# Batch-ahead routing and value sums collected by VectorE, in a recurrent block with attention and eight experts

## The chip, the cores and the metric

The kernel runs on one core of a Trainium2 chip. The metric is device time in microseconds. A core has TensorE (PE, with its weight loads shown as PEld), VectorE (DVE), ScalarE (ACT), GpSimd (POOL) and SyncE (SP), each with an instruction stream of its own; they meet at semaphores, and SyncE issues most of the transfers.

## The reference

Two layers on an input of 8 batches, 1024 positions and 256 features (8192 rows). Each layer is a sequence block times a gate, added to the input. The part that matters here is the gate of the second layer: attention with 16 heads of 8 dimensions within each batch, and a mixture of eight experts that routes each row to two of them.

```python
scores = jnp.einsum('bhsk,bhtk->bhst', Q[..., :KPH], K) / math.sqrt(KPH)
attn = jax.nn.softmax(scores, axis=-1)
ao = jnp.einsum('bhst,bhtv->bhsv', attn, V)
...
mla_out = ao @ o_w + o_b
probs = jax.nn.softmax(mla_out @ router_w + router_b, axis=-1)
topw, topi = jax.lax.top_k(probs, TOPK)          # TOPK = 2 of E = 8
topw = topw / (topw.sum(-1, keepdims=True) + 1e-08)
h1 = jnp.einsum('bsd,edf->ebsf', mla_out, w1) + b1[:, None, None, :]
h1 = jax.nn.gelu(h1, approximate=False)
h2 = jnp.einsum('ebsf,efd->ebsd', h1, w2) + b2[:, None, None, :]
moe_out = jnp.einsum('bse,ebsd->bsd', combine, h2)
```

The first layer's state-space scan and the second layer's delta rule are other stages of the same program; the change doesn't touch them.

## The kernel before

The program is a row of phases, each with a block of its own for every engine; one begins when the one before has ended. The phases in question are `attention` (from line 2008) and, within `experts`, `route` (from line 2356), followed by `compute` and `combine`.

**Attention** works in 32 units: a batch (8) times a group of four heads (4). Per unit PE makes twice the scores of four heads. First, the row maxima: 32 tiles of 128 queries by 1024 keys into the double-buffered `psM` (`maxima`, two matmuls of 512 columns each, L2172); VectorE reduces each to its maximum (`maximum`, L2321) and so frees the buffer. `minus_max` writes them as two parts, PE turns them (`turn`), ScalarE copies them (`turned`), SyncE puts them beside the queries, so that the second product is already reduced by the maximum. Then the scores themselves: 64 banks of 128 keys by 512 queries into three banks `psS` (`scores`, L2198); ScalarE exponentiates each into `probs` (`exponentials`, L2281) and so frees the bank. After each four banks PE adds `probs` times values into the one bank `psV` (`values`, L2211), in 16 groups of four, eight for each half of the queries. When a half is complete, `psV` is copied to `sums` (`collect`, L2286), and SyncE stores it (`store`). The next half's first `values` waits for `sums_ready`. The maxima run 8 tiles (`LEAD`) and one unit ahead of the scores. PE's order is fixed in `step`: for each s, maxima tile half 0, scores bank 2s, maxima half 1, scores bank 2s+1; after every second s the values of one group. ScalarE collects at position `MIDDLE` of a unit and at its end.

**Routing** takes 16 tiles of 512 rows, two to a batch. VectorE makes the inverse softmax sums (L2589), which go to memory and come back spread over the rows. Per tile SyncE fetches values and inverse sums (`values`, `inverses`, L2424, L2428), VectorE multiplies them (`tile`, L2602), PE turns the product and makes the logits (`tile`, L2548, L2550), ScalarE copies the turned rows (`tile`, L2500). Per batch: `choose` on VectorE (L2616 to L2635) makes the softmax, with the exponential by ScalarE (`exponential`, L2510), takes the two largest of eight and makes the mask; PE counts it (`ranks`, L2567, L2568); `spots` (L2641 to L2652) turns the counts into places `K.spot`; GpSimd scatters the rows there by 16 indirect transfers a batch (L2491). Beside it, one expert a batch, the weights are folded: SyncE fetches `raw1` and `raw2` (`weights_of`, 512 KB each, L2435, L2436), PE multiplies (`fold`: L2558 for the weights, 16 small products L2561 for the bias), ScalarE writes the heads (L2504, L2506) and VectorE the rests (L2606, L2608).

In each engine the order is written out. PE: two tiles, fold(b), ranks(b-1). ScalarE: two tiles, exponential(b-1), fold(b). VectorE: two tiles, fold(b-1), choose(b-1), spots(b-1). After the last batch VectorE makes the tables of expert tiles. SyncE has two raw buffers, so `weights_of(e)` from e = 2 waits for fold(e-2) of PE (`folded`) and VectorE (`rest2`).

## Time and profile before

| | us |
|---|---|
| median of 3 runs | 4166.02 |
| lowest, highest | 4165.89, 4167.23 |
| profiled execution, time | 4168.11 |
| profiled execution, span | 4166.5 |
| PE busy | 3502.2 (84%) |
| VectorE busy | 3253.8 (78%) |
| ScalarE busy | 2306.2 (55%) |
| GpSimd busy | 1369.6 (33%) |

The span is what the profile covers; the profiled execution's own time is 1.6 us above it. The busy time of an engine is the time in which it works on an instruction; the ends of matmuls are modelled, and matmuls of two kinds can overlap, so a busy PE is not a full PE. A timeline gives for each instruction, or a run of equal ones, the start, the time to the end of the run, and in brackets the idle time of the engine before it and what ended that. Such a releaser is inferred, and can be wrong where the named transfer had long landed.

### The profile page before, as it was taken

The page shows a single profiled execution, that of the slowest core. Times are in us where ns is not written, and L with a number is a line of the kernel's source. Part 1 is how long each engine was busy: PE and PEld are TensorE (multiplying, and loading weights), DVE is VectorE, ACT ScalarE, POOL GpSimd, SP SyncE. Part 2 cuts the span into 40 slices and gives each one's busy share as a digit, 9 for nine tenths or more (in the row PEclk, how much of TensorE's full clock was granted, in tenths as well). Part 3 has the DMA queues.
Part 4 walks back from the last instruction along what each step waited for, and adds up shares of the span by engine and source line. Part 5 has one row for each costly group of instructions (what it writes and reads, how often), then busy time and mean ns, then how long its engine had stood idle before and what let it go on. Part 6 is the DMA issues. An engine that isn't in the chain of part 4 may idle for free. (4 is left out here: it accounts for less than half of the span.)

```text
span 4166.5 us, 65564 instructions
## 1 busy us (share of the span) xinstructions
PE 3502.2 (84%) x20079; PEld 2104.2 (51%) x20080; DVE 3253.8 (78%) x4239; ACT 2306.2 (55%) x4128; POOL 1369.6 (33%) x905
## 2 busy tenths in 40 slices
PE   8969888888657979989799999999999965379950
PEld 3445555555346868878233333333333324279950
DVE  8959999999786645657889898989899823368868
ACT  6755555555594533311288888888888851033323
POOL 4448888889302445410000000000000004645530
PEclk9989999999888989999599999999999985589975
DMA  6665444454677943377123232322222114222348
GB/s 218 248 207 175 164 163 162 162 172 137 206 253 189 253 119 106 91 195 221 40 52 74 52 73 52 71 55 64 61 59 66 30 42 133 89 77 90 92 159 293
DMA packets 536067, 538.10 MB, mean 129 GB/s; under 512 B 85296, under 2 KB 441776, under 8 KB 535648
## 3 DMA queue, kind: packets, MB, share of 16 engines
q1 hardware_dynamic: 521856, 497.23, 40.8%
q0 software_dynamic: 13952, 37.74, 2.6%
q8 instruction: 123, 2.02, 0.2%
q14 instruction: 136, 1.11, 0.1%
HBM read 317.93 MB, written 215.71 MB: 128 GB/s over the span
## 5 line engine op out<-in xcount | busy, mean ns | idle before, releaser
L2321 DVE TENSOR_REDUCE at_top<-at_psM 128x1 f32<-128x1024 f32 x1024 | 1206.1, 1220 | 136.5 <-PE at_psM L2172 135.4
L2281 ACT ACTIVATE at_probs<-at_psS 128x512 f32<-128x512 f32 x2048 | 1060.9, 603 | 250.8 <-PE at_psS L2198 250.8
L2198 PE MATMUL at_psS<-at_q,at_k 64*128 64x512 f32 x2048 | 795.3, 468 | 8.3 <-ACT at_probs L2281 8.3
L575 POOL TENSOR_TENSOR sc_prod<-sc_state,sc_c_row 128x1024 f32<-128x1024 f32 x256 | 709.1, 2789 | 117.2 <-DVE sc_state L724 109.0
L2172 PE MATMUL at_psM<-at_k,at_q 62*128 62x512 f32 x2048 | 689.7, 451 | 36.5 <-DMA at_vraw<-scratch_vf 21.9
L724 DVE TENSOR_TENSOR_SCAN sc_state<-sc_dec,sc_psI 128x1024 f32<-128x1024 f32 x256 | 578.4, 2280 | 53.3 <-PE sc_psI L645 29.5
L2172 PEld LDWEIGHTS at_psM<-at_k,at_q 62*128 62x128 f32 x2048 | 313.1, 190 | 601.8 <-DVE at_top L2321 519.8
L2211 PE MATMUL at_psV<-at_probs,at_v 128*32 128x512 f32 x4096 | 546.3, 605 | 0.0
L656 PE MATMUL sc_psY<-sc_prod,sc_ident 128*128 128x512 f32 x1024 | 467.4, 597 | 3.5 <-DVE sc_y L710 2.2
L606 ACT ACTIVATE sc_dec<-sc_dt,sc_a_exp 128x1024 f32<-128x1024 f32 x256 | 293.6, 1148 | 311.1 <-DVE sc_state L724 308.3
L2198 PEld LDWEIGHTS at_psS<-at_q,at_k 64*128 64x128 f32 x2048 | 337.6, 184 | 195.5 <-ACT at_probs L2281 190.6
L2139 POOL COPY at_v<-at_vraw 128x256 f32<-128x256 f32 x32 | 12.9, 403 | 1253.1 <-DMA at_vraw<-scratch_vf 1169.4
L645 PE MATMUL sc_psI<-sc_diag,sc_uT 128*128 128x128 f32 x2048 | 266.9, 285 | 91.8 <-DVE sc_state L724 86.9
L645 PEld LDWEIGHTS sc_psI<-sc_diag,sc_uT 128*128 128x128 f32 x2048 | 245.6, 196 | 184.2 <-DVE sc_state L724 136.8
L656 PEld LDWEIGHTS sc_psY<-sc_prod,sc_ident 128*128 128x128 f32 x1024 | 185.6, 193 | 185.2 <-issue 173.1
L2765 POOL DMA_INDIRECT scratch_ys<-ex_y,ex_slot x156 | 172.0, 1103 | 185.1 <-DVE ex_y L2898 138.9
L2352 PEld LDWEIGHTS ex_psY<-ek_w,ex_hid 128*128 128x128 f32 x1872 | 223.8, 188 | 3.9 <-issue 1.0
L2352 PE MATMUL ex_psY<-ek_w,ex_hid 128*128 x1872 | 224.9, 279 | 0.6 <-DVE ex_hid L2891 0.6
L703 DVE TENSOR_TENSOR sc_psI<-sc_u,sc_b_row 128x1024 f32<-128x1024 f32 x128 | 171.1, 1337 | 8.7 <-ACT sc_uT L584 8.7
L2491 POOL DMA_INDIRECT scratch_xs<-er_rows,ek_spot x128 | 129.5, 1012 | 115.9 <-DVE ek_spot L2652 72.6
L592 ACT ACTIVATE sc_diag<-sc_ident,sc_b_col 128x128 f32<-128x128 f32 x512 | 161.7, 387 | 6.3 <-PE sc_psI L645 6.3
L2785 ACT ACTIVATE ex_xT<-ex_psT 128x512 fp32r<-128x512 f32 x39 | 23.4, 600 | 253.4 <-PE ex_psT L2815 253.4
(393 smaller groups left out, 4941.4 us busy)
## 6 DMA issues: line engine op xcount, KB each, us to landing
sc_c_row<-scratch_bc SPq DMA_DIRECT2D x128, 512.0 KB, 4.3
scratch_xs<-at_zeros SPq DMA_DIRECT2D x140, 264.0 KB, 4.7
sc_b_row<-scratch_bc SPq DMA_DIRECT2D x64, 512.0 KB, 5.1
ec_y<-scratch_ys SPq DMA_DIRECT2D x32, 512.0 KB, 6.4
ex_x<-scratch_xs SPq DMA_DIRECT2D x39, 264.0 KB, 3.1
si_x<-in_x SPq DMA_DIRECT2D x16, 512.0 KB, 4.4
scratch_xn<-si_xn SPq DMA_DIRECT2D x16, 512.0 KB, 5.1
scratch_x_t<-si_xT SPq DMA_DIRECT2D x16, 512.0 KB, 5.7
```

What stands on the lines that cost most here:

```text
L575: pool.tensor_tensor(prod[:, (n * H + h) % 8, :], state[slot][:], c_row[n % ROWS][:], ALU.mult).then_inc(prod_ready, 1)
L606: act.activation(dec[slot][:], dt[k][h][:], ACT.Exp, scale=a_exp[:, h, n:n + 1]).then_inc(dec_ready, 1)
L645: last = pe.matmul(psI[h][:, c, :], uT[k][h][:, c, :], diag[order % 2][:, c, :], start=True, stop=True)
L656: last = pe.matmul(psY[h][:, cols], ident[:], prod[:, own % 8, cols], start=(n == 0), stop=(n == S - 1))
L724: dve.tensor_tensor_scan(state[slot][:], dec[slot][:], psI[h][:].rearrange("p c t -> p (c t)"), 0.0, ALU.mult, ALU.add).then_inc(state_rea ...
L2172: ins = pe.matmul(psM[t % 2][:, half * TILE:(half + 1) * TILE], rows_of(q4[j], h, 0, MAXROW)[:, c * P:(c + 1) * P], rows_of(k4[j], h, 0, M ...
L2198: pe.matmul(psS[v % 3][:], rows_of(k4[j], h, 0, GROUP)[:, c * P:(c + 1) * P], rows_of(q4[j], h, 0, GROUP)[:, half * TILE:(half + 1) * TILE ...
L2211: last = pe.matmul(psV[32 * h:32 * h + 32, :], v4[j][:, c, h, :], probs[:, slot(j, at_slot[4 * g + n]), :], start=(c == 0), stop=(c == KC ...
L2281: act.activation(probs[:, slot(j, v), :], psS[v % 3][:], ACT.Exp).then_inc(act_done, 1)
L2321: dve.tensor_reduce(top[j % 2][:, h, c:c + 1], psM[t % 2][:], AX.X, ALU.max, negate=True).then_inc(maxed, 1)
L2352: last = pe.matmul(out, a, b, start=start and n == 0, stop=stop and n == len(parts) - 1)
L2765: pool.indirect_dma_start(out=A["ys"], out_offset=bass.IndirectOffsetOnAxis(ap=slot[par][:, s:s + 1], axis=0), in_=y[par][:, s, :], in_off ...
```

## The change

In attention, ScalarE's `collect` is taken out and given to VectorE, which does it ahead of maxima tile 26 (half 0, of the unit before) and tile 10 (half 1, of two units before), `COLLECTED`; the last three follow the loop. In routing, each engine turns the tiles of batch b+1 before batch b is chosen; PE's `fold` is split into the weights' product, ahead of ranks, and `fold_bias`, behind them; PE folds one batch later, ScalarE and VectorE two. There are three raw buffers instead of two. SyncE fetches the inverse sums of tiles 0 and 1 right after the first store of inverses, ahead of the first weights, and the later weights one tile later.

```diff
-    MIDDLE = at_slot[36]
+    COLLECTED = (18 + LEAD, FIRST + LEAD)
...
-                def collect(u, half):
-                    act.wait_ge(summed, u * GROUPS + (GROUPS + KC * (half + 1)))
-                    act.wait_ge(sums_st[half], u * QUAD * 16 + 16)
-                    act.activation(sums[half][:], psV[:], ACT.Copy).then_inc(sums_ready, 1)
...
-                            if e == MIDDLE:
-                                collect(u, 0)
...
-                        collect(u, 1)
...
+                def collect(u, half):
+                    dve.wait_ge(summed, u * GROUPS + (GROUPS + KC * (half + 1)))
+                    dve.wait_ge(sums_st[half], u * QUAD * 16 + 16)
+                    dve.tensor_copy(sums[half][:], psV[:]).then_inc(sums_ready, 1)
+
                 def unit(u, j):
                     for t in range(MT):
+                        for half in range(NHALF):
+                            back = half + 1
+                            if t == COLLECTED[half] and (not isinstance(u, int) or u >= back):
+                                collect(u - back, half)
                         maximum(u, j, t)
                     minus_max(u, j)
...
+                collect(UNITS - 2, 1)
+                collect(UNITS - 1, 0)
+                collect(UNITS - 1, 1)
...
+        RAWS = 3
...
                 def weights_of(e):
-                    if e >= 2:
-                        sp.wait_ge(folded, e - 1)
-                        sp.wait_ge(rest2, e - 1)
+                    if e >= RAWS:
+                        sp.wait_ge(folded, e - RAWS + 1)
+                        sp.wait_ge(rest2, e - RAWS + 1)
                         m.settle(sp)
...
                     if g == 0:
+                        inverses(0)
+                        inverses(1)
                         weights_of(0)
-                inverses(0)
-                inverses(1)
                 for i in range(2, NT):
                     sp.wait_ge(aon_ready, i - 1)
                     m.settle(sp)
                     values(i)
                     inverses(i)
-                    if i % 2 == 0:
+                    if i % 2 == 1:
                         weights_of(i // 2)
```

The order in routing on ScalarE:

```diff
+                tile(0)
+                tile(1)
                 for b in range(B):
-                    tile(b * NB)
-                    tile(b * NB + 1)
-                    if b:
-                        exponential(b - 1)
-                    fold(b)
-                exponential(B - 1)
+                    exponential(b)
+                    if b + 1 < B:
+                        tile((b + 1) * NB)
+                        tile((b + 1) * NB + 1)
+                    if b >= 2:
+                        fold(b - 2)
+                fold(B - 2)
+                fold(B - 1)
```

The order in routing on PE:

```diff
+                tile(0)
+                tile(1)
                 for b in range(B):
-                    tile(b * NB)
-                    tile(b * NB + 1)
-                    fold(b)
+                    if b + 1 < B:
+                        tile((b + 1) * NB)
+                        tile((b + 1) * NB + 1)
                     if b:
-                        ranks(b - 1)
-                ranks(B - 1)
+                        fold(b - 1)
+                    ranks(b)
+                    if b:
+                        fold_bias(b - 1)
+                fold(B - 1)
+                fold_bias(B - 1)
```

The order in routing on VectorE:

```diff
+                tile(0)
+                tile(1)
                 for b in range(B):
-                    tile(b * NB)
-                    tile(b * NB + 1)
-                    if b:
-                        fold(b - 1)
-                        choose(b - 1)
-                        spots(b - 1)
+                    if b + 1 < B:
+                        tile((b + 1) * NB)
+                        tile((b + 1) * NB + 1)
+                    choose(b)
+                    if b >= 2:
+                        fold(b - 2)
+                    spots(b)
+                fold(B - 2)
                 fold(B - 1)
-                choose(B - 1)
-                spots(B - 1)
```

## Rows read from the trace of the kernel before

**Rows 1.** Busy time by stretch (start:end, length, PE, PEld, DVE, ACT, POOL, clock, DMA).

```profile
3102.19:3144.39 42.20, 42.14 (x259) 15.11 (x258) 37.98 (x34) 34.26 (x68) 0.40 (x1) 1.00 0.25 62
...
3411.00:3665.00 254.00, 98.60 (x394) 81.07 (x394) 87.16 (x430) 23.50 (x42) 132.17 (x144) 0.52 0.37 110
```

**Rows 2.** Timeline of PE over two attention steps, the second with a collection.

```profile
2605.76 0.50 PE L2198 MATMUL at_psS<-at_q,at_k 64*128 64x512 f32 x1
...
2606.95 0.50 PE L2198 MATMUL at_psS<-at_q,at_k 64*128 64x512 f32 x1
2607.38 1.06 PE L2211 MATMUL at_psV<-at_probs,at_v 128*32 128x512 f32 x8
2608.38 0.49 PE L2172 MATMUL at_psM<-at_k,at_q 62*128 62x512 f32 x1
...
2611.07 0.49 PE L2172 MATMUL at_psM<-at_k,at_q 62*128 62x512 f32 x1
```

**Rows 3.** Timeline of ScalarE, the collection in the same steps.

```profile
2608.51 0.60 ACT L2286 ACTIVATE at_sums<-at_psV 128x512 f32<-128x512 f32 x1
```

**Rows 4.** Timeline of PE's weight loads in the first of these steps.

```profile
2606.33 0.18 PEld L2172 LDWEIGHTS at_psM<-at_k,at_q 62*128 62x128 f32 x1 [0.27 <-DVE at_top L2321]
...
2606.95 0.18 PEld L2198 LDWEIGHTS at_psS<-at_q,at_k 64*128 64x128 f32 x1 [0.33 <-ACT at_probs L2281]
```

**Rows 5.** Timeline of VectorE, the two maxima of that step.

```profile
2606.53 2.36 DVE L2321 TENSOR_REDUCE at_top<-at_psM 128x1 f32<-128x1024 f32 x2 [0.26 <-PE at_psM L2172]
```

**Rows 6.** Groups of instructions by line: count, busy us and mean ns of one.

```profile
L1759 DVE COPY dv_xt<-dv_ps 128x512 f32<-128x512 f32 x36 | 24.9, 691 | 27.9 <-PE dv_ps L1591 27.9
```

**Rows 7.** Waits in the routing stage: sum in us, times, longest.

```profile
POOL scratch_xs L2491 <- DVE ek_spot L2652: 72.6, 4, 44.2
...
POOL scratch_xs L2491 <- issue: 43.2, 124, 3.2
```

**Rows 8.** Timeline of GpSimd: the first scatter, and the first instruction after the last.

```profile
3459.61 1.35 POOL L2491 DMA_INDIRECT scratch_xs<-er_rows,ek_spot  x1 [44.18 <-DVE ek_spot L2652]
...
3663.92 0.21 POOL L155 MEMSET ex_ident<- 128x128 f32 x1 [3.13 <-POOLq L2420]
```

**Rows 9.** Timeline of VectorE in routing; last, one tile's instructions (ns; first, last start).

```profile
3433.44 1.33 DVE L2602 TENSOR_TENSOR er_aon<-er_ao 128x512 f32<-128x512 f32 x2 [6.18 <-DMA er_ao<-scratch_inv_sum]
...
3445.15 0.69 DVE L2602 TENSOR_TENSOR er_aon<-er_ao 128x512 f32<-128x512 f32 x1 [4.72 <-DMA er_ao<-scratch_inv_sum]
...
3447.49 0.22 DVE L2616 TENSOR_TENSOR er_lg<-er_psL,er_bias 128x64 f32<-128x64 f32 x1
...
3452.66 0.17 DVE L2635 COPY er_rows<-er_indexf 128x8 f32<-128x8 f32 x1
...
3477.26 0.22 DVE L2641 COPY er_chunk<-er_psA 128x64 f32<-128x64 f32 x1 [8.29 <-DMA scratch_x<-so_x]
...
3506.23 0.22 DVE L2621 TENSOR_REDUCE er_total<-er_ex 128x8 f32<-128x64 f32 x1 [22.83 <-ACT er_ex L2510]
...
L2652 DVE CAST ek_spot<-er_spot x8: 174/175/175, 3458.5 to 3636.8; 128x16 uint32<-128x16 f32 x8
```

**Rows 10.** Timeline of SyncE's transfers at the start of routing.

```profile
3422.35 0.59 SPq L2435 DMA_DIRECT2D er_raw<-in_w  x1
...
3426.37 1.46 SPq L2428 DMA_DIRECT2D er_ao<-scratch_inv_sum  x2
...
3438.00 0.66 SPq L2428 DMA_DIRECT2D er_ao<-scratch_inv_sum  x1
```

**Rows 11.** Timeline of PE in routing: first tile, fold, bias products, ranks.

```profile
3434.28 1.09 PE L2548 MATMUL er_psT<-er_ident,er_aon 128*128 128x128 f32 x4 [7.43 <-DVE er_aon L2602]
...
3439.18 3.67 PE L2558 MATMUL er_psW<-er_raw,er_foT 128*128 128x512 f32 x4
...
3451.84 3.41 PE L2561 MATMUL er_psB<-er_ob,er_raw 128*128 128x1 f32 x16
3455.11 0.67 PE L2567 MATMUL er_psA<-er_mask,er_before 128*128 128x64 f32 x2
```

More of the change, by code:

```diff
@@ L2367, in route @@
         foT, obw, wr, bias = m.sb("foT", [P, H, P]), m.sb("obw", [P, H, P]), m.sb("wr", [P, E]), m.sb("bias", [P, E])
-        raw1, raw2 = [m.sb(f"raw1{k}", [P, H, FF]) for k in two], [m.sb(f"raw2{k}", [P, FT, D]) for k in two]
+        RAWS = 3
+        raw1, raw2 = ([m.sb(f"{n}{k}", shape) for k in range(RAWS)] for n, shape in (("raw1", [P, H, FF]), ("raw2", [P, FT, D])))
         ao = [m.sb(f"ao{k}", [P, 2, TILE]) for k in two]
@@ L2390, in route @@
         weights, late, consts = m.sem("weights"), m.sem("late"), m.sem("consts")
-        ao_loaded, raw_loaded = [m.sem(f"ao_loaded{k}") for k in two], [m.sem(f"raw_loaded{k}") for k in two]
+        ao_loaded, raw_loaded = [m.sem(f"ao_loaded{k}") for k in two], [m.sem(f"raw_loaded{k}") for k in range(RAWS)]
         pe_fo, act_fo, pe_wr, act_wr = m.sem("pe_fo"), m.sem("act_fo"), m.sem("pe_wr"), m.sem("act_wr")
@@ L2430, in weights_of @@
                 def weights_of(e):
-                    if e >= 2:
-                        sp.wait_ge(folded, e - 1)
-                        sp.wait_ge(rest2, e - 1)
+                    if e >= RAWS:
+                        sp.wait_ge(folded, e - RAWS + 1)
+                        sp.wait_ge(rest2, e - RAWS + 1)
                         m.settle(sp)
-                    sp.dma_start(raw1[e % 2][:], w1_in[e, :, :, :]).then_inc(raw_loaded[e % 2], 16)
-                    sp.dma_start(raw2[e % 2][:], w2_in[e, :, :, :]).then_inc(raw_loaded[e % 2], 16)
+                    sp.dma_start(raw1[e % RAWS][:], w1_in[e, :, :, :]).then_inc(raw_loaded[e % RAWS], 16)
+                    sp.dma_start(raw2[e % RAWS][:], w2_in[e, :, :, :]).then_inc(raw_loaded[e % RAWS], 16)
                 for g in range(PARTS):
@@ L2504, in fold @@
                     act.activation(K.w1[0][:, e, :], psW[e % 2][:], ACT.Copy).then_inc(head1, 1)
-                    act.wait_ge(raw_loaded[e % 2], 32 * (e // 2 + 1))
-                    act.activation(flat(K.w2[0][:, e, :, :]), flat(raw2[e % 2][:]), ACT.Copy).then_inc(head2, 1)
+                    act.wait_ge(raw_loaded[e % RAWS], 32 * (e // RAWS + 1))
+                    act.activation(flat(K.w2[0][:, e, :, :]), flat(raw2[e % RAWS][:]), ACT.Copy).then_inc(head2, 1)
                 def exponential(b):
@@ L2553, in fold @@
                 def fold(e):
-                    pe.wait_ge(raw_loaded[e % 2], 32 * (e // 2 + 1))
+                    pe.wait_ge(raw_loaded[e % RAWS], 32 * (e // RAWS + 1))
                     if e >= 2:
@@ L2557, in fold, with fold_bias @@
                     for h in range(H):
-                        last = pe.matmul(psW[e % 2][:], foT[:, h, :], raw1[e % 2][:, h, :], start=(h == 0), stop=(h == H - 1))
+                        pe.matmul(psW[e % 2][:], foT[:, h, :], raw1[e % RAWS][:, h, :], start=(h == 0), stop=(h == H - 1))
+                def fold_bias(e):
                     for f in range(FT):
                         for h in range(H):
-                            last = pe.matmul(sums[:, e, f:f + 1], raw1[e % 2][:, h, f * P:(f + 1) * P], ob[:, h:h + 1],
+                            last = pe.matmul(sums[:, e, f:f + 1], raw1[e % RAWS][:, h, f * P:(f + 1) * P], ob[:, h:h + 1],
                                              start=(h == 0), stop=(h == H - 1))
@@ L2607, in fold @@
                     dve.wait_ge(head2, e + 1)
-                    dve.tensor_tensor(flat(K.w2[1][:, e, :, :]), flat(raw2[e % 2][:]),
+                    dve.tensor_tensor(flat(K.w2[1][:, e, :, :]), flat(raw2[e % RAWS][:]),
                                       flat(K.w2[0][:, e, :, :]).bitcast(F32), ALU.subtract).then_inc(rest2, 1)
```

## The prediction, made before the changed kernel was run

> **What bounds the kernel now.** I read first the busy time by stretch, to see which stages the change can reach, then in each stage the timelines of the engines and what ended each wait. Two stages are touched: attention (about 1997 to 3411 us) and routing (3411 to 3665 us) [rows 1]. In attention PE is busy throughout, VectorE for 37.98 and ScalarE for 34.26 of 42.20 us, so none of the helpers is full; PE counts as busy by modelled ends and overlapping matmuls, so its figure does not show the bound either. The repeating step does. One group of four score banks starts at 2605.76, the next at 2608.38: 2.62 us [rows 2]. Within it the fourth score matmul waits for ScalarE to free a bank [rows 4], the value matmuls follow it at 2607.38, and the next group starts 1.00 us later. So the loop is score, first exponential, fourth score, values. A step with a collection in it runs from 2608.38 to 2611.07, 2.69 us [rows 2]: the copy of 0.60 us does not quite fit ScalarE's gap [rows 3]. It costs 0.07 to 0.09 us, not 0.60.
>
> Routing is another picture: PE is busy for 98.6 of 254 us, VectorE 87.2, ScalarE 23.5, GpSimd 132.2 [rows 1]. GpSimd does 128 indirect scatters. Its waits are 43.2 us of spacing between scatters and 72.6 us for `K.spot` from VectorE, of which 44.2 lie before the first one and 28.4 later [rows 7]. From the first scatter at 3459.61 to 3663.92 less its last wait of 3.13 are 201.2 us [rows 8]; less 28.4 that is 172.8 us of GpSimd work, 21.6 a batch. The stage is the start of the scatters, plus this, plus starvation.
>
> **Attention: the collection goes to VectorE.** There are 64 collections. Taken from ScalarE they give back 64 x 0.08 = 5 us. On VectorE the nearest copy of that shape (128x512 from PSUM) takes 0.69 us [rows 6], while VectorE is idle for only 0.26 us in a step, between two pairs of maxima [rows 5]. The value matmuls end at about 2608.4, before the maxima of that step do (2608.89), so the collection finds its sums ready and pushes the next maxima back by 0.69 - 0.26 = 0.43 us, or about 0.35 if the instructions overlap a little, as two maxima of 1.22 in 2.36 us do. Queued behind it are these maxima; PE's second maximum tile of the next step waits for them (0.27 us of waiting as it is) and the scores are queued behind that. But the fourth score waits another 0.33 us for ScalarE anyway [rows 4]. The delay left on the loop is 0.43 - 0.33 = 0.10 at most and 0.02 at the low end; VectorE makes the rest good in the next gap. I take 0.04: net 64 x (0.04 - 0.08) = -3 us. The bounds: nothing stays (-5 us), or the pair of matmuls behind the delayed tile does not fit before the fourth score and 0.17 stays on each (+6 us). The values of the other half need `sums_ready` 1.6 us after the previous ones end, and the copy has ended by then; `store` and the fetch of the maxima rows on SyncE come 0.5 us later with a whole unit of room.
>
> The step lasts as long at the end of the stage, where VectorE has nothing to do; there the copy costs 0.09 us more than ScalarE's, once. On VectorE's price the Trainium skill (VectorE: DVE Perf Modes, The TRN2 errata) gives 120 + 512 cycles at 0.96 GHz, 0.66 us, against the 0.69 of the row; by it another 0.03 us per collection would vanish, 2 us in all.
>
> **Routing: the start.** Now the inverse sums for tiles 0 and 1 are issued at 3426.37, behind 1 MB of expert weights issued at 3422.35 [rows 10], and the first product waits until 3433.44 [rows 9]. With the two fetches put ahead of the weights and of three stores, I estimate 3430 for it: issue at about 3425 (they wait for the first store to land), two issues, and about 3.5 us for landing. Tiles 2 and 3 follow without new weights between them, at about 3437 instead of 3445.15. Choosing batch 0 needs no longer ScalarE's copies of tiles 2 and 3 nor the fold: 5.2 us (3447.49 to 3452.66 with the last copy) [rows 9], then ranks and `spots`, 3.6 us from 3455.11 to 3458.7 [rows 9, 11]. PE is through two tiles in 4.9 us each pair [rows 11], so ranks(0) comes at about 3444 and the first scatter at 3447.8, against 3459.6: -11.8 us. Bounds 3444 and 3452.
>
> **Routing: the rate.** Nominal chain before: from `spots(0)` to the tiles' products, VectorE's fold, choose, and PE's tiles 4.9 + fold 3.7 + bias sums 3.4 + ranks 1.1 [rows 11], then `spots`: about 16.4 us a batch. GpSimd needs 21.6, so it should never starve. It does, because the others crawl while it scatters: VectorE took up the ranks of batch 1 only at 3477.26 after 8.29 us of idle time, and waited 22.83 us for an exponential queued on ScalarE behind two row copies [rows 9]. `spots` left VectorE at 3458.7 for batch 0 and at 3637.0 for batch 7 [rows 9], 25.5 us a batch, so some 9 us a batch is stall. What stalls them the rows do not say; they show it only while scatters run.
>
> After the change the exponential is queued behind nothing of its own batch, ranks come before the bias sums, and the fold's sums come later: the stalls of PE and ScalarE are met with up to a batch of lead. Against this stands a new wait. `weights_of(e)` for e of 3 and more now stands on SyncE's queue ahead of the fetches of tiles 2e+2 and 2e+3, and waits for `rest2` of fold(e-3), which VectorE does in batch e-1, just before `spots`. The very next thing VectorE wants is tile 2e+2. So from batch 3 on the fetch is issued behind 1 MB of weights and VectorE waits for it: 1 us for the weights' issue, about 1.2 for the fetch, and 6.5 us landing, as tile 3 shows, issued 3438.00 to 3438.66 and used at 3445.15 [rows 9, 10]. That makes 9 us, then 1.3 for the products, 5.2 choose, 1.9 fold: about 17.8 us a batch. Still under 21.6, so by itself hidden, but it leaves little for stalls. The Trainium skill (DMA: Bandwidth & Descriptors, Issuing engines are not separate DMA queues) says that all issuers share the same 16 DMA engines; by that the scatters stretch this landing too, and the wait is nearer 10 than 9 us.
>
> Lead of `spots(b)` over GpSimd's need, worked forward from 3447.8: about 9, 15, 18, 21, 24, 26, 37 us for batches 1 to 7. If all of today's 9 us a batch stays (9, 18, 27, ... 63 us in sum), the worst shortfall is 28 us, as much as now. If half stays (4.5 a batch, 27 at batch 6), it is 1 us. I take 10 us, nearer the second, because the two worst stalls sit on work that gets a lead: -18 us.
>
> **The tail.** Behind `spots(7)` now stand two folds, 3.8 us, and PE's bias(6), fold(7), bias(7), 10.5 us, before the tables, some 25 short instructions that follow one another (0.17 us for 128x16 [rows 9], with their hand-over about 0.25), an estimated 6.5 us. Batch 7's scatters last 21.6, so these some 20 us fit, with nothing over; if PE crawls, up to 5 us come out. The third raw buffer costs nothing: it has no instruction.
>
> **Sum.** Routing -11.8 - 18 = -30, attention -3: -33 us. The profiled execution took 4168.11 us for a span of 4166.5, 2 us above the median of 4166.02 of three; I lay the difference on the median: **4133 us**.
>
> **Rivals.** (A) GpSimd becomes the bound: no starvation, start 3447.8 + 172.8 = 3620.6 against 3660.8, -40, with attention -5 and a start some us earlier -48: 4118 to 4122. For it: 16.4 and 17.8 are both under 21.6. Against: the stalls are bound to the scatters, which then never pause. (B) The stalls stay in full: only the start is won, -12 in routing, 4148 to 4154. For it: today's GpSimd pauses are where the others catch up, and they are gone. (C) Slower: the new wait of VectorE for tiles behind the weights, with stalls on top, sets the rate. It decides when a batch takes over 33 us from batch 3 on: five of these from 3473 put `spots(7)` at 3638 and the end past today's; at 34.5 us a batch it is 4176 with attention's bound of +3. The longest batch today, 33.7 us, speaks for it, the mean of 25.5 against. (D) The change doesn't do what it says: scatters start early, but attention pays 0.17 for each collection: 4142.
>
> **Chances.** Forecast with its surroundings (4124 to 4142, D included) 0.50; A 0.20; B 0.20; between B and no change 0.05; C 0.05. The range leaves out the outer half of A, C and the part between: 4117 to 4153. Within 0.2% (8 us, about what a measurement of this kernel can tell from no change) 0.05, slower 0.05, faster 0.90.
>
> **What would show it.** Attention: steps with a collection at 2.61 to 2.65 us, a VectorE copy of 0.69, units of 42.1 instead of 42.20. Routing: first scatter near 3447 minus what attention gained; GpSimd's waits for `K.spot` after the first near 10 us; VectorE waiting 4 to 6 us for `er_ao` in batches 3 to 6. I am wrong if the units grow past 42.4, if the scatters start after 3455, or if the engines' stalls grow with scatters that never pause.

## The result: 11 to 16 us less, where 33 were forecast

The changed kernel took 4152.88 us (median of 8 runs, 4147.69 to 4157.68) beside 4163.42 for the kernel before (8 runs, 4158.86 to 4167.23): a ratio of 0.9974, 95% interval 0.9963 to 0.9985. Two later comparisons of the same pair gave 0.9964 (0.9952 to 0.9977; 4120.21 against 4133.42) and 0.9961 (0.9947 to 0.9974; 4118.18 against 4132.59), a third 0.9964 (0.9953 to 0.9975; 4148.59 against 4162.05). So it is faster by 11 to 16 us.

The prediction was 4133 with a range of 4117 to 4153: the direction is right, and a third to a half of the forecast gain came. The time lies 0.12 us inside the range, which is luck, as the kernel before was 2.6 us faster beside it than when it was read for the prediction. What came is what rival B said: the start is won, the rate is not.

A set is a group of kernels that were run together; absolute times move by 30 us between sets, so times below are compared inside one set. That those sets differ in kind is a finding of its own, further down.

The profile after, in the order of the prediction. Its execution took 4155.52 us for a span of 4153.9. Attention first: VectorE's timeline in two steps of one group of four banks (start, duration, engine, line).

```profile
2606.27 2.36 DVE L2313 TENSOR_REDUCE at_top<-at_psM 128x1 f32<-128x1024 f32 x2 [0.26 <-PE at_psM L2172]
2608.55 0.68 DVE L2329 COPY at_sums<-at_psV 128x512 f32<-128x512 f32 x1
2609.14 4.71 DVE L2313 TENSOR_REDUCE at_top<-at_psM 128x1 f32<-128x1024 f32 x4
```

PE's timeline, the first maximum matmul of a step with a collection and that of the next:

```profile
2608.12 0.50 PE L2172 MATMUL at_psM<-at_k,at_q 62*128 62x512 f32 x1
...
2610.73 0.49 PE L2172 MATMUL at_psM<-at_k,at_q 62*128 62x512 f32 x1
```

The collection stands in VectorE's old gap, 0.68 us long, and four maxima follow it without a pause: VectorE makes the delay good, as forecast, and the step of 2.69 us [rows 2] is now 2.61. The Trainium skill (VectorE: DVE Perf Modes, The TRN2 errata) gives 120 + 512 cycles at 0.96 GHz for it, an estimate of 0.66 us; the median of all 64 is 0.681. The last maxima and collections end at 3405.85, before they ended at 3409.1. From its first maximum matmul attention takes 1407.5 us instead of 1412.3, 4.8 less; the stages ahead of it, which the change doesn't touch, took 1.5 us more in this execution.

Routing, busy time by stretch (columns as in [rows 1]), GpSimd's waits, its first scatter and first instruction behind the last, and `K.spot`'s eight writings (ns, first to last start):

```profile
3405.85:3655.60 249.75, 98.39 (x395) 80.49 (x395) 89.12 (x432) 23.83 (x42) 129.88 (x144) 0.54 0.38 113
```

```profile
POOL scratch_xs L2496 <- DVE ek_spot L2669: 69.2, 7, 33.2
POOL scratch_xs L2496 <- issue: 39.7, 121, 3.2
```

```profile
3445.32 1.34 POOL L2496 DMA_INDIRECT scratch_xs<-er_rows,ek_spot  x1 [33.19 <-DVE ek_spot L2669]
...
3651.39 0.20 POOL L155 MEMSET ex_ident<- 128x128 f32 x1 [3.09 <-POOLq L2425]
```

```profile
L2669 DVE CAST ek_spot<-er_spot x8: 174/175/176, 3444.2 to 3623.3; 128x16 uint32<-128x16 f32 x8
```

The sums are fetched at 3409.8 (3413.1 before); from there to the first scatter it is 35.5 us instead of 46.5, 11.0 less. But GpSimd's waits for `K.spot` behind the first scatter, called starvation here, are 69.2 - 33.2 = 36.0 us, and were 28.4 [rows 7]. From the first scatter to the end of GpSimd's work are 203.0 us (3651.39 - 3.09 - 3445.32), and were 201.2 [rows 8]. Of the two measures the second is the sounder: some stalls are put down to "issue" and not to `K.spot` (43.2 us of issue before, 39.7 after), so the rate got worse by 1.8 us and not by 7.6. The 18 us did not come.

What stands in the way now, by the sum of waits of VectorE, and PE's timeline in the middle of a batch of scatters:

```profile
DVE ek_w L2623 <- ACT ek_w L2509: 28.6, 5, 17.8
DVE er_chunk L2658 <- remote: 27.9, 3, 16.9
DVE er_aon L2619 <- DMA er_ao<-scratch_inv_sum: 26.3, 10, 6.2
```

```profile
3479.70 0.16 PE L2572 MATMUL er_psB<-er_ob,er_raw 128*128 128x1 f32 x1 [1.70 <-issue]
3482.53 0.16 PE L2572 MATMUL er_psB<-er_ob,er_raw 128*128 128x1 f32 x1 [2.66 <-issue]
3485.33 0.16 PE L2572 MATMUL er_psB<-er_ob,er_raw 128*128 128x1 f32 x1 [2.64 <-issue]
3488.13 0.16 PE L2572 MATMUL er_psB<-er_ob,er_raw 128*128 128x1 f32 x1 [2.64 <-issue]
```

VectorE's longest wait, 17.8 us, is for ScalarE's copy of a folded weight, and that copy waits for PE. PE for its part runs one bias product in 2.8 us, waiting for "issue", for nothing that the profile shows; 16 such products took 3.41 us together in [rows 11], before any scatter. This is what is called the crawl below.

### The profile page after: what moved, and what is told of

It is laid out like the page before. It is cut to its first block and busy times, and to the rows that moved or that the text cites. A ratio compares the mean times of both kernels' runs of the same rounds, so it can differ in the third digit from the quotient of the medians.

```text
span 4153.9 us, 65562 instructions
## 1 busy us (share of the span) xinstructions
PE 3496.1 (84%) x20079; PEld 2107.6 (51%) x20080; DVE 3288.6 (79%) x4303; ACT 2275.2 (55%) x4064; POOL 1366.7 (33%) x905
## 5 line engine op out<-in xcount | busy, mean ns | idle before, releaser
L2172 PE MATMUL at_psM<-at_k,at_q 62*128 62x512 f32 x2048 | 705.4, 454 | 41.3 <-DMA at_vraw<-scratch_vf 21.9
L724 DVE TENSOR_TENSOR_SCAN sc_state<-sc_dec,sc_psI 128x1024 f32<-128x1024 f32 x256 | 578.8, 2280 | 55.7 <-PE sc_psI L645 27.1
L2496 POOL DMA_INDIRECT scratch_xs<-er_rows,ek_spot x128 | 127.2, 994 | 109.0 <-DVE ek_spot L2669 69.2
```

Of the source, the lines that this page charges most:

```text
L724: dve.tensor_tensor_scan(state[slot][:], dec[slot][:], psI[h][:].rearrange("p c t -> p (c t)"), 0.0, ALU.mult, ALU.add).then_inc(state_rea ...
L2172: ins = pe.matmul(psM[t % 2][:, half * TILE:(half + 1) * TILE], rows_of(q4[j], h, 0, MAXROW)[:, c * P:(c + 1) * P], rows_of(k4[j], h, 0, M ...
```

## Experiments

**The two halves of the change.** `e1_attention` is the kernel before with the attention half of the diff (`COLLECTED` and `collect` on VectorE); `e2_routing` is the kernel before with the routing half. Each has its half of the diff of the change, so neither is shown again.

> The kernel before with the attention part of the change alone (value sums collected by VectorE). In the trace of after, attention from its first maximum matmul to the end of the last collection took 1407.5 us against 1412.3 before. Theory: the collection fits VectorE's gap and the wait that the fourth score has anyway, so this part alone gives about -5 us (-4 to -6). Rival: the shorter attention of that one trace is drift between executions, and the part is worth within 2 us of nothing.

> The kernel before with the routing part alone. Theory: the scatters start 11 us earlier, but starvation of GpSimd grows by 8 us (36 against 28.4 us of waits for K.spot behind the first), so it is worth -4 to -9 us. Rival: routing gains nothing or loses by itself, and the whole difference is attention's: 0 to +3 us.

Attention alone: 4149.62 against 4157.65, ratio 0.9986 (0.9976 to 0.9995), 5.8 us less. Routing alone: 4155.78, 0.9995 (0.9984 to 1.0007), 2 us less and not to be told from nothing. GpSimd waits 33.07 us ahead of its first scatter in e2's profile and 43.68 in e1's, which has the old routing. So the start is won (from the sums' fetch to the first scatter 35.4 us against 46.0) and the rate gives a part of it back: from first scatter to the end 193.8 us in e2, 190.4 in e1. That makes about 7 us less for routing; the interval of e2 reaches down to 6.7.

**The start alone.** `e5_inverses` moves the two fetches in the kernel before.

```diff
                     if g == 0:
+                        inverses(0)
+                        inverses(1)
                         weights_of(0)
-                inverses(0)
-                inverses(1)
```

> The kernel before with one step of the change: SyncE fetches the inverse sums of tiles 0 and 1 ahead of the first weights and the later stores. Theory: the first products come 4 to 5 us earlier; tile 3 still waits behind weights, so the first scatter comes about 3 us earlier, the rest unchanged: -2 to -4 us. Rival: the later waits for er_ao take it back, 0.

4158.21 against 4154.96, ratio 1.0008 (0.9994 to 1.0021): no gain to be seen, though the interval still holds the low end of what was expected, 2 us. GpSimd's first wait is 40.3 us in its profile, 3 to 4 less than in those of the old order (44.2 in [rows 8], 43.7 in e1). Whether these 3 us reach the end this run can't tell.

**Is it the place of the fold?** `e3_fold_behind` puts VectorE's `spots(b)` ahead of `fold(b - 2)`, so that ScalarE's late copy holds no spots up. `e6_two_ahead` turns tiles two batches ahead, has `spots(b)` directly behind `choose(b)`, and issues weights later on SyncE's queue.

```diff
                     choose(b)
+                    spots(b)
                     if b >= 2:
                         fold(b - 2)
-                    spots(b)
```

> The changed kernel, but VectorE does spots(b) before fold(b-2) instead of behind it. In the trace of after, VectorE waited 28.6 us in sum for ScalarE's fold with the places of a batch queued behind. Theory F (the fold's place): the starvation of 36 us comes from that wait; without it, it drops to under 15 us and the kernel to 10 to 20 us below the changed one. Theory S (every engine crawls while scatters run): the places wait for the ranks and the mask just as late; the kernel stays within 6 us of the changed one.

> The changed kernel with another order: tiles turned two batches ahead, VectorE does choose(b), spots(b), then the tiles of b+2, then fold(b-2); PE ranks(b) ahead of the tiles; the later weights are fetched one batch later on SyncE, so VectorE's products never queue behind them. Theory W (the new wait of VectorE for er_ao behind the weights, 2.5 to 6 us a batch, and ScalarE's fold ahead of the places cost the change its routing gain): starvation of GpSimd falls from 36 to under 15 us, 10 to 20 us below the changed kernel. Theory S (the crawl itself, a price per instruction while scatters run, whatever the order): starvation stays over 25 us and the kernel within 6 us of the changed one.

e3: 4153.76, 0.9989 (0.998 to 0.9999) of the kernel before, starvation 29.8 us. e6: 4147.96, 0.9985 (0.9976 to 0.9995), starvation 26.4. From first scatter to GpSimd's end they take 203.2 and 194.9 us, as the other kernels with the crawl (190.4 to 205.0). Neither order brings the forecast gain.

**Does the crawl need the scatters?** `e4_scatters_last` lets GpSimd wait for all spots before its first scatter.

```diff
                 for b in range(B):
-                    pool.wait_ge(spots_ready, b + 1)
-                    pool.wait_ge(rows_ready, (b + 1) * NB)
+                    pool.wait_ge(spots_ready, B)
+                    pool.wait_ge(rows_ready, B * NB)
```

> The changed kernel, but GpSimd waits for the places of all eight batches before it issues its first scatter; nothing else is different. Theory S (the crawl is tied to running scatters): places of batch 0 to places of batch 7 take about 106 to 115 us instead of 179, with no idle time of ScalarE over 15 us ahead of a row copy, and the kernel is slower by about 100 us because the scatters come last. Rival T (the crawl comes from something in the engines' own streams, such as the loading of straight-line code, whatever GpSimd does): they still take 165 us or more.

4226.64 us, as it must be with the scatters exposed. The row of `K.spot` and ScalarE's waits for the same stretch (3443 to 3548):

```profile
L2669 DVE CAST ek_spot<-er_spot x8: 174/174/175, 3442.8 to 3547.0; 128x16 uint32<-128x16 f32 x8
```

```profile
ACT er_rows L2505 <- PE er_psL L2559: 14.5, 10, 1.9
ACT ek_w L2509 <- PE er_psB L2572: 6.6, 1, 6.6
```

The same instructions in the same order need 104.2 us from the first to the last spots, where they needed 179.1 beside scatters; ScalarE's longest wait for a tile falls from 29.5 to 1.9 us. By itself this is one execution, and less clear than it looks. Its last 25 VectorE instructions ran from 3554.95 to 3564.1 with no idle time over 0.25 us between them although scatters had been going since 3548.07, and further down the same 106 us are reached with scatters running. What ties the crawl to the scatters is the two probes that have both in one execution, p1 and p3.

**The crawl by itself.** In `p1_probe` all of routing is done first. Then VectorE runs 1000 one-element copies and ScalarE a short loop of activations, while GpSimd goes through memsets, plain transfers and three kinds of scatters.

```diff
+                idle(16)
+                for i in range(24):
+                    pool.dma_start(A["kt"][i, :, :], rows[:, i, 0:P]).then_inc(probe_st, 16)
+                idle(16)
+                for i in range(24):
+                    scatter(i, A["vf"], P)
+                idle(16)
+                for i in range(12):
+                    scatter(i, A["vd"], P)
+                    idle(2)
...
+                for i in range(24):
+                    scatter(i, A["kd"].rearrange("n (a c) -> (n a) c", c=4), 4)
```

> A measurement, not a version: the changed kernel with all its scatters after the places of the last batch, and before them, when the other engines are done, a stretch in which GpSimd in turn idles, issues 24 plain transfers, idles, 24 indirect scatters of 512-byte rows, idles, 12 of them with a pause between, idles, 24 scatters of 16-byte rows, idles. Meanwhile VectorE runs 1000 copies of one element written out one after the other, without a wait, and ScalarE 600 copies of 128x128 in a loop with one wait a turn. Theory L (the crawl is late delivery of written-out code while scatters run): VectorE's copies go at one per 0.1 us or so and at 0.5 to 1 us each in the stretch of indirect scatters, ScalarE's loop keeps its pace throughout. Rival M (semaphores or memory are slow under scatters): ScalarE's loop with its waits slows as well, or VectorE's copies, that have no semaphores, do not slow. Theory I (it is the indirect transfers): nothing slows in the stretch of plain transfers.

VectorE's copies by stretch (start:end, length, busy us and count, clock, DMA share, GB/s): memsets, plain transfers, scatters back to back, scatters with 1.1 us of memsets behind each (here its copies ran out); and three rows of its timeline inside the third:

```profile
3565.74:3575.00 9.26, 9.26 (x155) 0.50 0.01 2
3575.29:3588.10 12.81, 12.81 (x215) 0.50 0.35 114
...
3597.70:3627.90 30.20, 7.85 (x93) 0.50 0.15 50
...
3637.50:3664.60 27.10, 16.22 (x269) 0.50 0.08 28
```

```profile
3604.70 0.28 DVE L2760 COPY er_junk_v<-er_ones 128x1 f32<-128x1 f32 x3 [1.13 <-issue]
3606.13 0.27 DVE L2760 COPY er_junk_v<-er_ones 128x1 f32<-128x1 f32 x3 [1.16 <-issue]
3607.55 0.28 DVE L2760 COPY er_junk_v<-er_ones 128x1 f32<-128x1 f32 x3 [1.15 <-issue]
```

16.8 copies per us beside memsets, and as many beside plain transfers at 114 GB/s; 3.1 beside scatters at 50 GB/s, in clumps of three, later single ones, 0.70 or 1.40 us apart. It begins some 3 us after the first scatter begins and ends some 3.5 us after the last has ended. ScalarE's loop by stretch, beside memsets, scatters of 512 bytes a row, and scatters of 16 bytes a row:

```profile
3588.10:3597.40 9.30, 8.98 (x41) 0.50 0.05 15
3597.70:3627.90 30.20, 15.14 (x67) 0.50 0.15 50
...
3675.30:3705.50 30.20, 16.98 (x76) 0.50 0.03 2
```

ScalarE falls from 4.4 to 2.2 and 2.5 activations per us, at 50 GB/s and at 2. So the bytes are not the cause, and the crawl doesn't need written-out code, since a loop crawls too: theory L as it was put has failed. With a break behind each scatter ScalarE kept its pace as well (116 in 27.1 us).

The Trainium skill (SBUF — State Buffer, SBUF: two separate sides) says that of the engines' ports into SBUF only the pair shared by VectorE and GpSimd is contended and that PE and ScalarE never wait on anyone. Here PE and ScalarE crawl as VectorE does, so that by that page this is not a matter of those ports. The Trainium skill (Runtime: NRT & Kernel Launch, Instruction fetch mechanics) has code streamed in blocks of 256 instructions at a mostly hidden cost. That the cost is hidden agrees with 2800 copies in one run without a gap (169.47 us, below); the trace shows the transfers with 8 KB each.

**Breaks between scatters.** `p2_pauses` has other breaks, both engines' code written out; `e8_paced`, `e9_paced_ahead` and `e10_before_paced` put one tiny memset and a wait behind each of the first 112 scatters of the changed kernel, of e6 and of the kernel before.

```diff
                                 in_=rows[:, c, :], in_offset=None).then_inc(scattered, 16)
+                            if b + 1 < B:
+                                pauses.append(0)
+                                pool.memset(pause[:], 0.0).then_inc(paused, 1)
+                                pool.wait_ge(paused, len(pauses))
```

> The crawl by itself, again. All of routing is done before GpSimd scatters; then VectorE runs 2800 one-element copies and ScalarE 800 one-element activations, written out with no wait, while GpSimd goes through stretches with 9 us of memsets between them: 20 scatters with a tiny memset and a wait behind each; 20 with a memset of 0.56 us behind each; 24 with 1.4 us of memsets behind every fourth; 24 with the same behind every sixth; then the real scatters without a pause. The first probe showed VectorE at 16.8 copies per us beside memsets or plain transfers from GpSimd, at 3.1 beside scatters 1.27 us apart (down to one copy in 0.70 or 1.40 us) and undisturbed beside scatters 2.37 us apart; it began some 3 us after the first scatter and ended some 3 us after the last. Theory Q (something behind the scatters fills up, and the other engines' instructions wait only when it is full; it takes a scatter in more than 1.27 and less than 2.37 us): with 0.56 us behind each scatter (period about 1.85 us) over 14 copies per us, and groups of four clearly above 3.1. Theory D (the engines are held in proportion to the scatters' share of the time): about 0.69 x 3.1 + 0.31 x 16.8 = 7 copies per us at 0.56 us, about 6 in groups of four. Which holds decides whether short pauses between scatters can pay in the changed kernel.

> The changed kernel unaltered, so that the kernels with pauses are compared with it on the same chip. Both theories: within noise of its earlier ratio to the kernel before, 0.9974 (0.9963 to 0.9985).

> The changed kernel with one tiny memset and a wait for it on GpSimd behind each scatter of the first seven batches: a scatter begins 1.36 us instead of 1.27 us after the one before (0.09 x 112 = 10 us more GpSimd work), and nothing else is altered. In the second probe VectorE (2800 copies) and ScalarE (800 activations) ran without one stall beside scatters 1.36 us apart, and beside groups of six with 1.4 us behind each. Theory Q (the crawl comes only when scatters follow each other without a break for some 3 us or more): VectorE needs some 15 us a batch as it did with the scatters held to the end (104.2 / 7), less than the 21.8 us that GpSimd now needs, so that the 36 us in which GpSimd starved for spots fall to under 5: 31 less, 10 more, 20 to 24 us under the changed kernel; first scatter to end of GpSimd about 180 to 185 us instead of 203. Theory R (the crawl needs real routing work, or any run of scatters, and the probe's written-out code escaped it by chance): starvation stays near 30 us and the time is 0 to 10 us above the changed kernel.

> The same pauses in the version of e6_two_ahead (tiles turned two batches ahead of the choice, spots ahead of weights). Theory Q: with the crawl gone GpSimd is the bound in either order of the work, so this is within 4 us of e8_paced. If the lead itself pays once the crawl is gone, it is over 5 us below e8_paced. Theory R: as e6_two_ahead (0.9985 of the kernel before) or up to 10 us slower.

> The kernel before with the same pauses and nothing of the change. Theory Q: its routing is slowed by the same crawl (12 to 28 us of starvation between the profiles of its kind), so it gains most of that less 10 us: 5 to 18 us below the kernel before; and the change, compared between e8_paced and this kernel, is then worth its start and attention (some 11 + 5 us). Theory R: 0 to 10 us above the kernel before.

```profile
3564.16 169.47 DVE L2771 CAST er_junk_v<-er_ones 128x1 bf16<-128x1 f32 x2800
```

That is VectorE's timeline in p2: 2800 copies beside every kind of break, groups of six scatters back to back among them, without one stall. It looked like a cure, but p2 had no stretch of scatters back to back beside which the copies could have crawled (they had run out before the real scatters), and the kernel before took 4135.3 us beside it, as in the sets without the crawl (below). The kernels of the next set: after_again 4120.21 (0.9964), e8 4130.33 (0.9993), e9 4130.24 (0.9996), e10 4149.33 (1.0035), the kernel before 4133.42. The pauses cost the changed kernel 10.1 us, exactly their price, and win nothing, where 20 to 24 us less were expected; in e10 they cost 15.9, 6 over the price, which stays unexplained. With pauses in both, the change is worth 19.0 us (e10 to e8). after_again's profile says why the pauses win nothing:

```profile
POOL scratch_xs L2496 <- issue: 41.4, 126, 3.3
POOL scratch_xs L2496 <- DVE ek_spot L2669: 33.3, 2, 33.0
```

```profile
L2669 DVE CAST ek_spot<-er_spot x8: 174/174/405, 3443.6 to 3550.2; 128x16 uint32<-128x16 f32 x8
```

The same program that starved for 36.0 us starves here for 0.3, and its spots take 106.6 us instead of 179.1: as in e4, but with the scatters running. The crawl isn't always there. Where the kernel before takes 4133 to 4135 us no kernel shows it; where it takes 4155 to 4163, each kernel that chooses while it scatters does. Of the 35.7 us between the spans of after and after_again, 31.4 lie between the first scatter and GpSimd's end (203.0 and 171.6 us). Theory Q was not tested in this set.

These profiles also show the engines' own pace. In after_again the first two batches of spots come 12.7 and 12.2 us apart and those of batches 3 to 6 17.1 to 18.9, for VectorE now waits up to 6.2 us for `er_ao`: the 17.8 us of the prediction. The old order in e10 needs 13.7 us a batch, less than the 16.4 of the prediction. So without the crawl the change makes the engines slower, and this is hidden under GpSimd's 21.6.

**Both in one execution.** `p3_both` holds scatters back to back and three kinds of breaks; beside it ran e8's kernel, the changed kernel and the kernel before.

> The probe with unpaused and paused scatters in one execution: VectorE runs 2800 one-element copies written out while GpSimd goes through 24 scatters back to back (1.27 us apart), 20 with a tiny memset and a wait behind each (1.36), 20 with a memset of 0.56 us (1.79), and 24 with 1.4 us behind every fourth, with 9 us of memsets between the stretches. Theory C (the crawl is a matter of the chip or of the moment: some have it, some not, whatever the kernel): if the kernel before takes some 4155 us or more here, the first stretch crawls (some 3 copies per us for most of it); if it takes some 4135 us or less, no stretch crawls, the first neither. Theory Q (the break between scatters decides, on every chip): the first stretch crawls and the three others run at 16 to 17 copies per us, whatever the kernel before takes. If C holds and the first stretch crawls, the other three say whether a pause cures it.

> e8_paced again: the changed kernel with a tiny memset and a wait behind each of its first 112 scatters. On a chip without the crawl it costs its 10 us and gains nothing, as e8_paced did (10 us above the changed kernel). On a chip with the crawl: if pauses of 0.09 us cure it, 15 to 25 us under after_3; if not, 0 to 10 us above.

> The changed kernel unaltered. Theory C: where the kernel before takes some 4155 us or more, starvation of 25 to 40 us behind the first scatter and a ratio near 0.9974; where it takes some 4135 us, starvation under 3 us and a ratio near 0.9964, as in after_again.

> The kernel before, profiled on the same chip as the others. Theory C: on a chip without the crawl its starvation behind the first scatter is under 4 us too (it was 28 in the profile that the prediction read), so that the change has no rate to win there and gains its start (11 us) and its attention (5 us) alone; on a chip with the crawl it is 12 to 30 us, about what the changed kernel shows beside it.

This set had the crawl (kernel before 4162.05). VectorE's copies in p3 by stretch: back to back (1.27 us from one to the next), tiny memset (1.36), memset of 0.56 us (1.79), groups of four with 1.1 us of memsets:

```profile
3574.90:3605.20 30.30, 8.44 (x99) 0.50 0.15 50
...
3614.80:3641.70 26.90, 9.49 (x113) 0.50 0.14 47
...
3651.20:3686.20 35.00, 35.00 (x581) 0.50 0.11 38
...
3696.30:3732.00 35.70, 32.34 (x518) 0.50 0.13 43
```

3.3, 4.2, 16.6 and 14.5 copies per us: a period of 1.36 us crawls, 1.79 doesn't, and groups of four (6.18 us, 1.55 on average) lose 0.55 us each. Beside the real scatters behind them, without a break, VectorE crawls again, at 3.7 in the 43.6 us from their start, so that the two good stretches are not a crawl that had gone away:

```profile
3743.40:3787.00 43.60, 13.34 (x163) 0.50 0.16 53
```

Theory D, a share of time, would have 7 copies per us at 1.79 and is out; the crawl sets in somewhere between 1.36 and 1.79 us. Theory Q is right in its main point, that the break decides, and wrong for the smallest break, where it expected 16 to 17 copies and 4.2 came. Theory C is right that the crawl isn't always there.

Late transfers of code are an obvious rival. The queue that brings instructions (count, MB, share of the DMA engines' time), in the stretch back to back and in that of 1.79 us:

```profile
q14 instruction: 2, 0.02, 0.2%
...
q14 instruction: 9, 0.07, 0.7%
```

The two transfers took 0.3 and 0.5 us, the nine 0.3 to 0.6, so the blocks themselves are not late. But VectorE's copies ran on for 46 instructions (3.2 us) after the first scatter and ScalarE's activations for 49 (4.9 us): alike in instructions and not in time, as if each engine lived on a small stock that was then refilled late. In the two later stretches that crawl it was 81 and 82 instructions. That is a hint and not tested.

paced_2 took 4143.91 (0.9952, 0.9939 to 0.9964), after_3 4148.59: pauses of 0.09 us now bring 4.7 us instead of costing 10.1, between the two outcomes that were expected (15 to 25 less, or 0 to 10 more). The intervals of the two ratios overlap, the runs hardly do (4136.85 to 4147.82, 4146.77 to 4153.78). GpSimd's waits in before_2, then after_3, then paced_2:

```profile
POOL scratch_xs L2491 <- DVE ek_spot L2652: 76.0, 7, 43.3
```

```profile
POOL scratch_xs L2496 <- DVE ek_spot L2669: 71.6, 8, 32.9
```

```profile
POOL scratch_xs L2497 <- DVE ek_spot L2674: 51.5, 3, 33.7
```

Starvation 32.7, 38.7 and 17.8 us; from first scatter to GpSimd's end 201.7, 205.0 and 197.7. The difference of 11.7 us between the spans of before_2 (4163.8) and after_3 (4152.1) falls into: -3.3 up to the fetch of the sums (3411.8 and 3408.5; attention itself 4.9 less, the stages ahead of it 1.6 more), start -10.4 (45.7 and 35.3 us to the first scatter), rate +3.2, the rest -1.2.

**Longer breaks in the kernel.** `grouped` puts two memsets of 0.56 us behind every fourth scatter of the first four batches.

> The changed kernel with two memsets of 0.56 us and waits for them on GpSimd behind every fourth scatter of the first four batches, nothing else altered. Price: in p3_both four scatters with this break took 6.18 us against 5.09, so 16 breaks cost 17.5 us. In that probe VectorE ran 518 copies in 35.7 us beside such groups, 14.5 per us against 16.8 undisturbed, where scatters back to back left it 3.3. The work of the other engines for seven batches took 104 us with scatters held back; at 14.5 / 16.8 of that pace it is done in about 120 us, within the first five batches of scatters (24.7 us each with breaks). Where the crawl is there (kernel before at some 4155 us or more): starvation behind the first scatter under 8 us instead of 36 to 39, and 8 to 15 us below after_4. Where it isn't (before at some 4135 us): 14 to 18 us above after_4, the price alone. Rival (real routing work crawls by something else than the scatters' spacing): starvation stays above 20 us, and the time is 0 to 18 us above after_4 on a chip with the crawl.

> The changed kernel unaltered, beside grouped. By the earlier jobs its ratio to the kernel before is 0.9964 on either kind of chip (14.9 us of 4133, 13.5 of 4162), and its starvation 33 to 39 us where the crawl is there and under 3 us where it isn't.

This set was without the crawl (before 4132.59): grouped 4136.65 (1.0009, 1.0 to 1.0018), after_4 4118.18 (0.9961), 18.5 us apart, the price that was worked out as 17.5. What such breaks bring where the crawl is there was thus not measured. This set and that of e5, e6 and p1, which had the crawl, have the same chip number on record, 0. If it is the same chip, the chip alone does not decide.

## Why the prediction was off

- **Attention** (-3, bounds -5 to +6): right in mechanism, a little small. From its first maximum matmul to the last collection it takes 1412.1 to 1412.9 us in the five profiles of the old order and 1406.3 to 1408.1 in the twelve of the new: 5 us less, 0.08 a collection, which is all that ScalarE was to give back. So VectorE's delay cost the loop nothing to speak of. The -5.8 us of e1 (interval -10 to -2) agree.
- **Start** (-11.8, first scatter at 3447.8): right. -11.0, -10.6 and -10.4 in three pairs of profiles (before and after, e1 and e2, before_2 and after_3). The first scatter came at 3445.32, with the sums fetched 3.3 us earlier.
- **GpSimd's own work** (172.8 us): right. after_4 needed 172.9 us from first scatter to end (3442.32 to 3615.20), after_again 171.6.
- **Rate** (-18, "I take 10 us, nearer the second, because the two worst stalls sit on work that gets a lead"): this is the step that failed. It has starvation fall from 28.4 to 10 us. Measured, from first scatter to GpSimd's end, are +1.8, +3.4 and +3.2 us in the three pairs of profiles with the crawl; without it there is next to nothing to win. Two errors are in it. The stalls were laid to certain instructions that had been late, when the instructions of PE, ScalarE and VectorE were late whichever they were; a lead of a batch moves work to another place in the queue, and there it crawls too. The worst waits only changed their names: 22.83 us for an exponential [rows 9] became 29.50 for a row copy and 17.77 for a fold. And "they show it only while scatters run" was read off correctly and stands in the rivals and the signs of being wrong, but not in the sum. Rival B's outcome came. Its reason, "today's GpSimd pauses are where the others catch up", fits p3, where breaks give VectorE its pace back; in the kernel itself it was not tested.
- **One execution taken for the kernel.** 28.4 us of starvation was a term of the sum. The same old routing took from first scatter to GpSimd's end 201.2 us in the profile that the prediction read, 190.4 in e1's, 191.9 in e5's and 201.7 in before_2's: 18 to 29 us above the 172.8 of GpSimd's own work. With tiny pauses (e10, in a set without the crawl) its waits for spots behind the first scatter were 1.7 us. Where the crawl is absent, the change gains start and attention alone: 11.8 + 3 = 14.8 us by those two terms of the forecast, 13.2 and 14.4 measured between medians, 15 to 16 by the ratios.
- **The new wait** for tiles behind the weights: there, 5.7 and 6.2 us at a time, as forecast, and so are 17.1 to 18.9 us a batch in after_again. Without the crawl it is hidden under GpSimd; what part it has beside the crawl was not measured. Rival C did not come: it wanted over 33 us a batch from batch 3 on, and in after's profile the spots of batches 2 to 7 come 25.4 us apart on average, though the largest distances between two batches are 39.6 and 35.8.
- **The tail** (0 to 5 us): from GpSimd's end to the end of the span it is 505.7 us before and 505.6 after, 504.6 in before_2 and 503.3 in after_3; nothing came out.

With 0.20 on rival B and 0.50 on the forecast, the chances were the wrong way round for a bound cause ("what stalls them the rows do not say"): a gain that rests on an unexplained stall going away deserved the smaller one.

## What to carry to other kernels

When several engines at once are late for "issue", a lead may not help, and here neither one batch nor two did; first find what runs at that time, by holding it back (here scatters held to the end: 104 us of work instead of 179) and by having it run and pause within one execution, as the effect can be absent in another. Price a change by what it does to the start and to the bound engine, and count on nothing from a stall whose cause the profile does not name. Before a stall of one profile becomes a term of a sum, look at it in a second profile, taken at another time.

## What the runs showed of the hardware

- In the sets with the crawl: while GpSimd issues indirect scatters 1.27 to 1.36 us apart, single instructions or clumps of a few of VectorE and ScalarE start only every 0.70 or 1.40 us, and PE's every 2.8 us (after). In the probes it began some 3 us into it for VectorE, 5 for ScalarE and 11 for ScalarE's loop, and ended some 3.5 us behind the last scatter. At 1.79 us apart (16.6 copies per us) it is gone, with 1.1 us of memsets behind every fourth (14.5) nearly so. Plain transfers that GpSimd issues 0.5 us apart don't cause it (16.8), and 16 bytes per row are as bad as 512 (ScalarE at 2.5 and 2.2 activations per us, 4.4 undisturbed).
- It is present in some sets of runs and absent in others, for the same program: spots in 179.1 and 169.2 us (after, after_3) or 106.6 and 105.0 (after_again, after_4), the kernel before 4155 to 4163 or 4133 to 4135 us. Whether that is a matter of the chip, of its surroundings or of how the program was loaded stays open, and so does the path on which instructions and scatters meet.
- In p3 the transfers that bring code took 0.3 to 0.6 us each with the crawl and without it; they are not what is late.
- Beside VectorE's 2800 copies scatters kept their 1.27 us (p3): there the scatters were not slowed in turn.
